# One sequence of the memory layer started in the attention before it, one pair of the next attention started in the memory's last sequence, and the PSUM banks of both numbered anew

## The reference, cut to what matters

```python
x = x + _L2_attn_ref(_layernorm(x), ...)
x = x + _L2_xattn_ref(_layernorm(x), ctx, ...)   # "L2x"
x = x + _L2_ffn_ref(_layernorm(x), ...)          # "L2f", a memory of product keys
x = x + _L3_attn_ref(_layernorm(x), ...)         # "L3a", grouped-query attention
```

```python
h = act(hidden @ W_up.T + b_up) @ W_down.T + b_down      # 256 -> 1024 -> 128
q = (h @ W_q.T), split in 2 x 8 heads x 64
sim = q . keys                                           # 2 x 8 heads x 45 keys
sx, sy = top_k(sim, 8); all = sx[:, None] + sy[None, :]
sc, pk = top_k(all, 8)                                   # 8 of the 2025 slots
z = act((h . down_embed[idx]) * softmax(sc))
out = sum over heads and k of z * up_embed[idx]          # 2025 x 256
```

## Time and profile before

| | us |
|---|---|
| Median of 3 runs | 2177.07 (2170.6 to 2178.75) |
| The profiled execution's own time | 2179.06 |
| Its span, first to last instruction | 2177.3 |
| TensorE busy | 1871.7 (86%) |
| VectorE busy | 1489.5 (68%) |
| ScalarE busy | 1076.5 (49%) |
| GpSimd busy | 1080.2 (50%) |
| Mean granted TensorE clock | 0.937 of full |

### The profile page before, as it was taken

The page is one execution under the profiler, slowest core; times in us unless marked ns, Lnnn a source line. Parts: engine busy times, 40 slices in busy tenths (PEclk is TensorE's granted clock), DMA queues, the critical chain, the costliest instruction groups (busy, mean ns, idle before and its releaser), DMA issues.

```text
span 2177.3 us, 31816 instructions
## 1 busy us (share of the span) xinstructions
PE 1871.7 (86%) x11438; PEld 1379.7 (63%) x11438; DVE 1489.5 (68%) x2537; ACT 1076.5 (49%) x2335; POOL 1080.2 (50%) x789
## 2 busy tenths in 40 slices
PE   7577689799799896899999999678888789887999
PEld 6111157545789874677777777567777555445888
DVE  5698943465764585777777776489999858665543
ACT  4444422244222364666666666467666546534443
POOL 2599931120890173755555554499999800012221
PEclk9688989599899998999999999889999989998999
DMA  4111002030400010100000001000000020000000
GB/s 158 46 34 34 0 1 71 5 155 0 175 1 1 1 31 20 59 14 1 1 1 1 1 1 39 19 1 1 1 1 28 0 80 1 1 0 1 6 9 8
DMA packets 22173, 54.96 MB, mean 25 GB/s; under 512 B 8463, under 2 KB 13752, under 8 KB 19592
## 3 DMA queue, kind: packets, MB, share of 16 engines
q1 hardware_dynamic: 22024, 53.01, 7.3%
HBM read 44.61 MB, written 1.05 MB: 21 GB/s over the span
## 4 chain that ended last, share of the span: by engine, by line
PE 57%; DVE 16%; POOL 10%; issue 7%; ACT 7%; SPq 1%; DMA 0%; DVEq 0%; POOLq 0%; ACTq 0%
POOL sbuf L1306 4%; PE psum L4084 4%; DVE sbuf L2270 3%; PE psum L4145 3%; PE psum L4217 2%; PE psum L3466 2%; POOL sbuf L1314 2%; PE psum L4570 1%; PE psum L4591 1%; PE psum L4577 1%; PE psum L4116 1%; PE psum L4132 1%; PE psum L4088 1%; PE psum L4096 1%; PE psum L4320 1%
## 5 line engine op out<-in xcount | busy, mean ns | idle before, releaser
L1306 POOL TENSOR_TENSOR sbuf<-sbuf 128x1035 f32<-128x1035 f32 x128 | 248.3, 1968 | 0.9 <-ACT sbuf L1927 0.9
L4217 PE MATMUL psum<-sbuf 128*128 128x128 f32 (+1 forms) x1024 | 143.7, 291 | 58.3 <-ACT sbuf L1936 42.2
L1936 ACT ACTIVATE sbuf<-sbuf 128x1001 f32<-128x1001 f32 (+1 forms) x128 | 141.6, 1139 | 101.0 <-DVE sbuf L3059 65.7
L4217 PEld LDWEIGHTS psum<-sbuf 128*128 128x128 f32 (+1 forms) x1024 | 125.6, 152 | 79.3 <-ACT sbuf L1936 58.5
L1261 POOL TENSOR_TENSOR sbuf<-sbuf 128x512 f32<-128x512 f32 x64 | 66.7, 1042 | 187.2 <-DVE sbuf L2947 187.2
L1107 POOL TENSOR_TENSOR sbuf<-sbuf 128x1024 f32<-128x1024 f32 x64 | 149.9, 2355 | 15.7 <-DVE sbuf L2270 14.9
L2270 DVE TENSOR_TENSOR_SCAN sbuf<-psum,sbuf 128x1024 f32<-128x1024 f32 x64 | 144.6, 2278 | 13.6 <-ACT psum L1427 6.9
L3414 PE MATMUL psum<-sbuf 96*128 96x512 bf16 x256 | 84.0, 439 | 75.1 <-DVE sbuf L2270 32.3
L1860 ACT ACTIVATE sbuf<-psum,sbuf 128x128 f32<-128x128 f32 x256 | 90.4, 365 | 107.3 <-DVE sbuf L2941 107.3
L3051 DVE SCALAR_TENSOR_TENSOR psum<-sbuf,psum 128x1024 f32<-128x1024 f32 (+1 forms) x96 | 122.4, 1275 | 14.6 <-PE psum L4207 7.0
L1427 ACT ACTIVATE psum<-psum,sbuf 128x1016 f32<-128x1016 f32 x64 | 68.9, 1081 | 125.1 <-PE psum L3414 125.1
(11 more groups left out here) (879 smaller groups left out, 5135.1 us busy)
## 6 DMA issues: line engine op xcount, KB each, us to landing
sbuf<-sbuf SPq DMA_DIRECT2D x42, 128.0 KB, 2.4
sbuf<-w_p_d SPq DMA_DIRECT2D x8, 512.0 KB, 3.9
sbuf<-w_qkv_d SPq DMA_DIRECT2D x3, 768.0 KB, 4.4
sbuf<-w_e_d SPq DMA_DIRECT2D x1, 2048.0 KB, 7.8
sbuf<-w_gu_d SPq DMA_DIRECT2D x1, 2048.0 KB, 9.8
sbuf<-w_gu_d SPq DMA_DIRECT2D x2, 1024.0 KB, 7.8
sbuf<-w_dn_d SPq DMA_DIRECT2D x1, 2048.0 KB, 17.5
sbuf<-w_q_d SPq DMA_DIRECT2D x1, 2048.0 KB, 8.1
```

Of the source, the lines that this page charges most:

```text
L1306: pool.tensor_tensor(P_r[g % 7][:, :, :], rows.unsqueeze(2).to_broadcast([128, 23, 45]), cols.unsqueeze(1).to_broadcast([128, 23, 45]), AL ...
L1936: act.activation(Q_r[g % 6][:, 0:w], Q_r[g % 6][:, 0:w], ACT.Silu, scale=q8_p[n % 2][:, h:h + 1]).then_inc(silu_done, 1)
L4217: last = pe.matmul(Gps[0:m, c, :], Q_r[g % 6][:, 128 * c:128 * c + m], ident[:, :], start=h == 0 and c % 4 == 0, stop=h == 7, skip_group_c ...
```

## The change

Three things.

1. **L2f's front for sequence 0 goes into L2x's loop.** Statistics at round 56, u at 57 (VectorE); deviation at 56 (ScalarE); transposes at 58 (TensorE, into L2x's own scratch) and the copy at 59 (ScalarE). The statistics and u of sequence 1 go to rounds 60 and 62. The up-projection is cut in two: blocks 0 to 3 at the end of round 63, blocks 4 to 7 in round 64 before the output projection of item 61. SiLU follows in halves in rounds 64 and 65, around the copy of the last probabilities. Down-projection and query stand in round 66 ahead of the last output projection. The wait of TensorE on L2x's last residual now stands behind the similarities. The table load in `L2f_rstd` is left out for sequences 0 and 1.
2. **L3a's front for sequence 0 goes into L2f's sequence 7**, and L2f's end into L3a's first two pairs. On VectorE the constants, memsets and statistics of sequence 0 stand at s = 2, u at 4, statistics of sequence 1 at 8, the keys at 13; on ScalarE a table load and the deviation at 3, the copy at 6, q's bias at 10; on TensorE the transposes at 5, q and k at 9, v at 14. The loop of L3a then begins with scores(0); `L2f_out(7, 0)` stands in pair 0 and `L2f_out(7, 1)` in pair 1, each behind the scores; `L2f_resid(7)` in pair 1 behind the subtraction, and TensorE waits for it there.
3. **Banks and places.** L2f: z from 0 to 3072, `pro` from 3072 to 0. L3a: score buffers to 1024 and 2048, transposes to 3072, front to 0 and 512. In SBUF the keys and the value buffer of L3a move to places that are free while L2f still runs.

The diff, cut to the order of the steps (the helpers that move are the same, but for what is shown):

```diff
-        zps = view(psum, 0, [1024])
+        zps = view(psum, 3072, [1024])
-        pro = view(psum, 3072, [1024])
+        pro = view(psum, 0, [1024])
-        L3a_S = [view(psum, 1024 * p, [8, 128]) for p in range(2)]
-        L3a_pT = view(psum, 2048, [8, 128])
-        L3a_front = view(psum, 3072, [512])
+        L3a_S = [view(psum, 1024 + 1024 * p, [8, 128]) for p in range(2)]
+        L3a_pT = view(psum, 3072, [8, 128])
+        L3a_front = view(psum, 0, [512])
...
# ScalarE, L2x's loop over i
+                if i == 59:
+                    L2f_unT(0)
...
+                if i == 56:
+                    L2f_rstd(0)
+                if i == 60:
+                    L2f_rstd(1)
+                if i == 64:
+                    L2f_he(0, 0, 4)
+                if i == 65:
+                    L2f_he(0, 4, 8)
-            act.wait_ge(resid_done, L2x_start['resid'] + 8)
-            L2f_rstd(0)
-            L2f_unT(0)
-            L2f_rstd(1)
-            L2f_he(0)
# ScalarE, L2f's loop over n and s
+                    if n == 7 and s == 3:
+                        act.preload_act_table_set('natural_log_exp_and_others')
+                        L3a_rstd(0)
+                    if n == 7 and s == 6:
+                        L3a_unT(0)
+                    if n == 7 and s == 10:
+                        act.wait_ge(L3a_w_loaded, 128)
+                        L3a_qTc(0)
-            act.wait_ge(resid_done, L2f_start['resid'] + 8)
             act.preload_act_table_set('natural_log_exp_and_others')
-            L3a_rstd(0)
-            L3a_unT(0)
             L3a_rstd(1)
-            L3a_qTc(0)
# VectorE, L2x's loop, L2f's loop, L3a's loop
+                if i == 56:
+                    L2f_stats(0)
+                if i == 57:
+                    L2f_u(0)
+                if i == 60:
+                    L2f_stats(1)
+                if i == 62:
+                    L2f_u(1)
...
+                    if n == 7 and s == 2:
+                        dve.tensor_reduce(L3a_mask4[:, :], ...)
+                        for p in range(3):
+                            dve.memset(L3a_vg[p][:, :, 8:9], 1.0)
+                            dve.memset(L3a_vg[p][:, :, 9:32], 0.0)
+                        L3a_stats(0)
+                    if n == 7 and s == 4:
+                        L3a_u(0)
+                    if n == 7 and s == 8:
+                        L3a_stats(1)
+                    if n == 7 and s == 13:
+                        L3a_keys(0)
-            L2f_resid(7)
-            dve.wait_ge(resid_done, L2f_start['resid'] + 8)
+            L3a_values(0)
             for p in range(38):
                 if p < 32:
                     L3a_max(p)
                     L3a_sub(p)
+                if p == 0:
+                    L3a_u(1)
+                if p == 1:
+                    L2f_resid(7)
# TensorE, L2x's loop
+                if i == 64:
+                    L2f_up(0, 4, 8)
+                if i == 66:
+                    L2f_down(0)
+                    L2f_query(0)
                 if i >= 3:
                     L2x_proj(i - 3)
                 if i < 64:
                     L2x_qkTr(i)
...
+                if i == 58:
+                    L2f_uT(0)
+                if i == 63:
+                    pe.wait_ge(L2f_w_loaded, 128)
+                    L2f_up(0, 0, 4)
-            pe.wait_ge(resid_done, L2x_start['resid'] + 8)
-            pe.wait_ge(L2f_w_loaded, 128)
-            L2f_uT(0)
-            L2f_up(0)
-            L2f_down(0)
-            L2f_query(0)
             L2f_sims(0)
+            pe.wait_ge(resid_done, L2x_start['resid'] + 8)
             L2f_z(0, 0)
# TensorE, L2f's loop and L3a's loop
+                    if n == 7 and s == 5:
+                        L3a_uTr(0)
+                    if n == 7 and s == 9:
+                        L3a_qk(0)
+                    if n == 7 and s == 14:
+                        pe.wait_ge(resid_done, L2f_start['resid'] + 7)
+                        L3a_value(0)
...
             L2f_acc(126)
             L2f_acc(127)
-            L2f_out(7, 0)
-            L2f_out(7, 1)
-            pe.wait_ge(resid_done, L2f_start['resid'] + 8)
-            L3a_uTr(0)
-            L3a_qk(0)
-            L3a_value(0)
+            pe.wait_ge(mask_done, L2f_start['mask'] + 128)
+            pe.wait_ge(prod_done, L2f_start['prod'] + 96)
             for p in range(38):
                 if p < 32:
                     L3a_scores(p)
+                if p == 0:
+                    pe.wait_ge(vc_done, L3a_start['vc'] + 1)
+                    L2f_out(7, 0)
+                if p == 1:
+                    L2f_out(7, 1)
+                    pe.wait_ge(resid_done, L2f_start['resid'] + 8)
                 if s == 0 and n < 7:
                     L3a_uTr(n + 1)
```

More of the change, by code:

```diff
@@ L4313, in L3a_scores, with L2f_z, L2f_acc @@
                 last.then_inc(score_done, 1)
+            def L2f_z(n, half):
+                if n > 0 or half > 0:
+                    pe.wait_ge(mask_done, L2f_start['mask'] + 16 * n + 8 * half)
+                for c in range(2):
+                    e = 1024 * half + 512 * c
+                    m = min(512, 2025 - e)
+                    last = pe.matmul(zps[:, 512 * c:512 * c + m], h2T_p[n % 2][:, :], de[:, e:e + m], start=True, stop=True)
+                last.then_inc(z_done, 1)
+            def L2f_acc(g):
+                half, h = g // 8 % 2, g % 8
+                pe.wait_ge(silu_done, L2f_start['silu'] + g + 1)
+                for c in range(8):
+                    if h == 0 and g > 0 and c % 4 == 0:
+                        pe.wait_ge(gt_done, g // 4 - 1 + c // 4)
+                    m = 105 if half == 1 and c == 7 else 128
+                    last = pe.matmul(Gps[0:m, c, :], Q_r[g % 6][:, 128 * c:128 * c + m], ident[:, :], start=h == 0 and c % 4 == 0, stop=h == 7, skip_group_check=True, is_transpose=True)
+                last.then_inc(sum_done, 1)
@@ new lines, in L2f_out @@
+            def L2f_out(n, part):
+                pe.wait_ge(gt_done, 4 * n + 4)
+                if n < 6:
+                    pe.wait_ge(simc_done, n + 3)
+                for c in range(8 * part, 8 * part + 8):
+                    m = 105 if c == 15 else 128
+                    last = pe.matmul(pro[:, 512:768], GT[0:m, c, :], ue[0:m, c, :], start=c == 0, stop=c == 15)
+                if part == 1:
+                    last.then_inc(proj_done, 1)
+            L2f_sims(0)
+            pe.wait_ge(resid_done, L2x_start['resid'] + 8)
```

303 lines of the change are left out of this document (138 added, 165 removed).

## The result

The changed kernel takes 2146.1 us (median of 4 runs, 2143.89 to 2149.61) where the kernel before takes 2173.84 on the same chip (4 runs, 2170.39 to 2178.75). The ratio is 0.986, with a 95% interval of 0.9838 to 0.9882. That is 27.7 us less by the medians (their quotient is 0.987, inside the interval), where the prediction has 28.8. The profiled execution took 2144.78, its span 2143.1.

What follows compares the result with a forecast made beforehand. GpSimd and VectorE hold L2f's loop; in the stretches on its two sides one sequence goes step after step. Gains 16.3 + 12.5, banks 0, make 28.8 us: 2177.07 to 2148.3, stated as 2148.5, range 2140 to 2160.

Steps and rivals of the forecast that it cites:

- Norm inside the rounds: L2x's rounds 56 to 62: L2f's layer norm costs 0.25 us, only for its transposes; bounds 0 to 1.0.
- Up-projection: L2f's, in two halves in L2x's drain: first half +0.3 us, second makes item 61's projection 1.4 later.
- Last projection: L2x's last output projection: start moves from 1368.21 to 1370.65, duration falls from 2.48 to 1.48 us.
- Behind it: After L2x's last projection: similarities, 2.03 us, and their copy with hand-over, 0.8; top-8 starts at 1375.0.
- First half: L2f's sequence 7, first half: 1.8 us of added VectorE work costs 0, covered by the wait for z.
- Table loads: Two on ScalarE at slot 3 of sequence 7, 1.28 us each: cost 0; with no slack 3.1.
- Second half: L2f's sequence 7, second half: VectorE has no gap, so statistics and keys cost 2.1 us; bounds 0.6 to 4.
- End of the last accumulation to fourth maximum: Join of L2f and L3a: 17.8 us, so the fourth pair's maximum starts at 1764.8 instead of 1777.34.
- The banks' case: Rival: masks in L2f's loop slow by 0.43 us each, loop 55 us longer, time 2203; chance 0.03.
- the half case: Rival: waits left in place hold a front back, one gain of two goes, 2161 to 2165; chance 0.06.
- Sequence 7 did not pay: Rival: L2f's sequence 7 pays for its added work, about 6 us in all, time 2154; chance 0.12.
- The clock's case: Rival: TensorE's clock falls in L2x's drain and behind `L2f_out(7, 1)`, losing 7.0 and 3.5 us, 2159; chance 0.13.

Runs made afterwards that it cites:

- e11: The changed kernel run once more without any edit; 2147.52 us, ratio 0.9854 to the kernel before.
- e1: The kernel before with only the new banks and places, every step where it was; ratio 1.0008 to the kernel before.
- e2: The changed kernel with L3a's front and L2f's end back in their old order; ratio 0.9903 to the kernel before.
- e9: The changed kernel with L2f's up-projection, SiLU, down-projection and query back behind L2x's last residual, only the layer norm staying early; ratio 0.9945 to the kernel before.
- e6: The changed kernel with two extra unread VectorE operations of 1024 columns in slot 2 of sequence 7, its first half; 2147.92 us, one run.
- e4: The changed kernel with L3a's first keys and sequence 1's statistics moved behind VectorE's last product of sequence 7; ratio 0.9858 to the kernel before.
- e3: The changed kernel with L2f's front put back behind L2x's last residual; ratio 0.9949 to the kernel before.

## Why the prediction was right

**Part 1, 16.3 predicted, 17.4 measured** (17.4 again in e11). The 17.4 are against an A of 40.67 before; against the 42.29 of e1 they would be 19.0.
- *Norm inside the rounds, 0.25:* the round with the transposes took 7.88 instead of 7.67 between two norms of q and k, in the change, e2, e9 and e11 alike, and no other round moved: 0.2.
- *Up-projection, +0.3 and +1.4:* too dear. The probabilities' transposes started 4.54 after the norm, as before, so the first half cost 0; item 61's projection started 0.43 late (8.64 for 8.21 after the norm), and item 62's not at all (13.40 both times). I had charged full durations for groups that run into each other: 2.03 in the timeline, 1.80 in the chain.
- *Last projection, +2.44, at 1.48:* it came 1.44 later and took 1.47. This is the 1.0 that the part gained beyond the forecast, all of it from the step before.
- *Behind it,* 4.35 predicted, 4.24 measured.
- *Residual +1.5:* +0.45, for the same reason and the shorter projection.

**Part 2, 12.5 predicted, 10.5 in the first profile, 13.5 in e11.**
- *First half, 0, with the wait shrinking to 2.5:* B was 22.04 for 22.09, so the number is right and the reason only half. The wait shrank to 1.07. The prediction laid the end of the masks (1721.0) beside the end of the accumulation, and left GpSimd's product where it was, though that product needs a mask: it now waits 1.42 for one, and the SiLU on which z hangs came 1.44 later. What paid for it was accumulation and z at full clock, 1.10 + 1.85 for 1.97 + 2.52, which the prediction did not see. That is no single case: all nine executions with the new order here and without e6's load had z at 1.85, all three with the old order (before, e1, e2) at 2.49 to 2.53. Why the level is higher there is not shown. e6 shows that no cover is left. 1.6 of what was put in is u(0) waiting for GpSimd; the 1.8 of the prediction had all these operations at their durations beside nothing, while the trace of before had u at up to 1.83.
- *Table loads, hidden, 1.28 each:* so. The second is followed by SiLU at once (1688.83 + 1.28, 1690.12); no drain is seen. The estimate of 2150 rested on the drain that the Trainium skill's page "ScalarE: Activation LUTs", section "What ACT_TABLE_LOAD costs", adds to each switch; here the next function starts 0.01 to 0.02 after the load, and the measurement decides.
- *Second half, +2.1:* C grew by 1.65, and e4 gives 1.56 of it back: it is the keys and the statistics.
- *End of the last accumulation to fourth maximum, 17.8:* 17.4 in e11 (1747.93 − 1730.51), 19.5 in the first profile (1741.12 − 1721.58).
- *Banks, 0:* e1.

**The rivals.** The banks' case and the half case are out by e1 to e3. Sequence 7 did not pay in time, though e6 shows that its cover was thinner than I had it. The clock's case was right in kind for one of its two stretches: in the first profile the low level around the last accumulation cost 2.95 of the 3.5 that the case had there. But it began behind the 1.51 idle ahead of the last accumulation, not behind `L2f_out(7, 1)` where the case had its gap: that one was 0.52, and the transposes after it ran at 1.04. In L2x's drain the low level never came with the new order. By its own test the prediction was wrong in the first profile, since it named a low clock in these stretches as a sign against it, and right in e11. The level there changes from one execution to the next of one program, so it belonged into the range and not among the cases.

The total is right partly by luck. In the first profile the errors compensate: +1.1 in part 1, +0.5 in the second half, +0.4 behind it, −2.95 of clock, 27.9 in all. In e11 the clock's share is missing, and the two parts give 17.4 + 13.5 = 30.9, more than the 28.8; its medians differ by 31.4. The mechanism, a front taken off the path and its matmuls into TensorE's waits, is what e2 and e3 show part by part.

## What to carry to other kernels

A front that runs step after step between two loops can be worth most of its length: here 17.4 of the 20.1 us between the last residual and the top-8. The layer norm was 3.4 us of it, the matmuls moved ahead of the last residual the rest. It takes buffers that are free while the loop before still runs. An idle stretch of an engine ahead of a wait is cover only for work that doesn't stand before what releases that wait: follow the wait back to the engine itself before you fill it. And before a clock level in one profile is made a cause, take the same kernel's profile twice.

## What was not expected of the hardware

- Three kinds of VectorE operation with their tensors in SBUF waited for a running GpSimd operation and then did their own work: `tensor_scalar` took 2.02 for 0.40, `scalar_tensor_tensor` 2.16, `tensor_tensor` of 1024 columns up to 3.37 for 1.22. GpSimd's product took 3.26 where VectorE was first. Statistics (0.42) and operations with an operand in PSUM (1.20 to 1.29) did not wait. An operation's price therefore has to be read in the neighbourhood that it moves into.
- The granted clock behind equal idle stretches of TensorE (1.24, 0.60, 1.51 us, and 1.23, 0.60, 1.51) was low in one execution and full in the next of the same program. The Trainium skill's "TensorE: Matmul & The Clock Gate", section "HAM oscillation", ties the drop to idle gaps between bursts; the drops here did begin behind gaps, but a gap of the same length did not bring one each time.
